# Causal attention on one core: a group's four score products in a row, the next job's maxima products in one lump behind them

## The chip, the cores and the metric

The kernel runs on one core of a Trainium2 chip. The metric is the device time of one execution in microseconds (us), as the median of several. TensorE (PE in the rows) has two columns of work in the trace, the matmuls (PE) and the weight loads (PEld); VectorE is DVE, ScalarE is ACT, GpSimd is POOL, and SyncE (SP) issues most transfers.

## What is computed

The reference is a small transformer: differential causal attention over x of 2 x 1024 x 128 (16 heads, each with two score maps), a routed feed-forward block, a second attention inside each token, and the feed-forward block again. The change is in the first attention only:

```
att = jnp.einsum('bhtd,bhsd->bhts', q, k) * (1.0 / math.sqrt(hd))
causal = jnp.tril(jnp.ones((T, T), dtype=bool))
att = jnp.where(causal, att, -jnp.inf)
att = jax.nn.softmax(att, axis=-1)
...
att = att[:, :, 0] - lambda_full * att[:, :, 1]
out = jnp.einsum('bhts,bhsd->bhtd', att, v)
```

## The kernel before

The program is a row of phases: `phase_a1` (projections), `phase_a2` (the first attention), `phase_a3`, `phase_f`, `phase_b` (the second attention) and `phase_f` again. Each phase begins when the one ahead of it is done. Within a phase every engine has its own list of instructions, written out by hand and run in that order; engines meet only at semaphores.

`phase_a2` does 16 **jobs**, one for each set of four score maps (index hh, 0 to 3) and batch element. A job needs the maximum of each score row before it can take exponentials, so the scores are computed twice. One pass, with queries on the partitions, gives the maxima (function `maximum_scores`, L449, with a product that adds the causal mask, L453); VectorE reduces it (L564). The negated maxima are split in three bf16 parts by GpSimd (`split`) and turned on TensorE (`maximum_rows`, L462), and VectorE adds them to the queries' tile as extra rows (L580). The other pass, with keys on the partitions, gives scores that have the maximum taken off already (`scores`, L492). ScalarE takes their exponential (L547), GpSimd clears the upper triangle of diagonal blocks (L384), and `values` (L505) multiplies them with v, four maps side by side in four column strips of the array. ScalarE copies the sums (L537), TensorE turns them (`turn`, L471), VectorE divides (L592, L594), and GpSimd combines.

A job has G = 12 **groups**, called at 0 to 11 here: four blocks of 128 keys for the first 512 queries, then eight for the second 512. A group is four score products, one for each hh, and one call of `values`, for the group before it. The score products have 512, 384, 256, 128 columns in groups 0 to 3, 512 in groups 4 to 8, then 384, 256 and 128. `scores` uses three PSUM banks in turn (ST_SLOTS = 3), so a product waits until the exponential three products back is done:

```
if s >= ST_SLOTS:
    pe.wait_ge(exp_done.sem, s - ST_SLOTS + 1)
```

The passes for later jobs are cut in **items**: 24 units of maxima for a job, u0 to u23 (u0 to u7 cover two maps each, with 128 to 512 columns for each; u8 to u23 cover one map with 640, 768, 896 or 1024 columns), one item of rows, and one turn. A job's list (`items`) has 26: u7 to u12 of the next job, the turn of the job before, u13 to u23, then u0 to u4 of the job after next, the rows, u5 and u6. Items use two pairs of PSUM banks in turn, so an item waits until VectorE is done with the item two back:

```
if i >= 2:
    pe.wait_ge(item_taken.sem, i - 1)
```

The loop of the tensor block that the diff touches deals the items out among the score products. VectorE takes the items in the same order, and makes the next keys' tiles (`pad`, L573) between them.

Of the kernel before, what the change touches and what calls it, by code (L numbers as in the profile page):

```python
# [301 lines left out]
def phase_a2(nc, rows_q, rows_k, rq, rk_of_group, rk, v1, att, k, queries_spread, keys_spread):  # L302
# [5 lines left out]
    with ExitStack() as ctx:  # L308
# [12 lines left out]
        U, G = len(units), len(groups)  # L321
        STEPS = 4 * G
# [21 lines left out]
        def items(n):  # L344

            later = [("max", n + 1, u) for u in range(0 if n < 0 else EARLY, U) if n + 1 < JOBS]
            if n >= 1:
                later.insert(min(TURN_ITEM, len(later)), ("turn", n - 1, 0))
            early = [("max", n + 2, u) for u in range(EARLY) if n + 2 < JOBS]
            if n + 1 < JOBS:  # L350
                early.insert(min(EARLY_ROWS, len(early)), ("rows", n + 1, 0))
            return later + early
# [80 lines left out]
        def _(pe):  # L433
# [40 lines left out]
            def item(kind, n, u):  # L474
                if kind == "max":
                    maximum_scores(n, u)
                elif kind == "rows":
                    maximum_rows(n)
                else:
                    turn(n)  # L480

            def scores(n, at, hh):
                g, b = n // BATCH, n % BATCH
                half, sbk = groups[at]
                s = STEPS * n + 4 * at + hh
                if at == 0 and hh == 0:
                    pe.wait_ge(rows_added.sem, n + 1)
                if s >= ST_SLOTS:
                    pe.wait_ge(exp_done.sem, s - ST_SLOTS + 1)
                lo, hi = queries_of(half, sbk)  # L490
                dst = ps[:, ST_BANK + s % ST_SLOTS]
                nc.tensor.matmul(dst[:, 0:hi - lo], rk[:, n % 3, hh, sbk * P:(sbk + 1) * P], rq[:, g, b, lo:hi],  # L492
                                 start=True, stop=True).then_inc(st_psum.sem, 1)

            def values(n, at):
                g, b = n // BATCH, n % BATCH
                half, sbk = groups[at]
                pe.wait_ge(exp_done.sem, exp_done.at(n, 4 * at + 4))
                if at in DIAGONAL:
                    pe.wait_ge(masked.sem, masked.at(n, DIAGONAL.index(at) + 1))  # L500
                if sbk == 0 and (n >= 1 or half == 1):
                    pe.wait_ge(o_copied.sem, 2 * n + half)
                lo, hi = queries_of(half, sbk)
                for hh in range(4):
                    last = nc.tensor.matmul(ps[32 * hh:32 * hh + 32, O_BANK, lo - 512 * half:512],  # L505
                                            v1[:, b * NT + sbk, 2 * g + hh // 2, :], ex[:, (G * n + at) % 3, hh, 0:hi - lo],
                                            start=sbk == 0, stop=sbk == (3 if half == 0 else NT - 1))
                last.then_inc(values_done.sem, 1)
# [4 lines left out]
            for n in range(JOBS):  # L513
                todo = items(n)
                given = 0
                for at in range(G):
                    for hh in range(4):
                        scores(n, at, hh)
                        while given < len(todo) and given * STEPS < (4 * at + hh + 1) * len(todo):
                            if todo[given][0] == "turn" and at < 2:  # L520
                                break
                            item(*todo[given])
                            given += 1
                    if at >= 1:
                        values(n, at - 1)
                    elif n >= 1:
                        values(n - 1, G - 1)
# [797 lines left out]
```

## Time and profile before

| what | value |
|---|---|
| median of 3 runs | 2138.11 us (2136.7 to 2138.21) |
| the profiled execution | 2138.5 us, its span 2136.7 us |
| busy over the span: PE, DVE, POOL, ACT | 86%, 88%, 66%, 52% |
| `phase_a2`'s jobs 0 to 14 | about 87 to 556 us of the span |
| job 15 of `phase_a2` | about 556 to 585 us |
| `phase_b` | about 700 to 2090 us |

The page's shares are means over stages with different limits. In `phase_b` VectorE is busy 99% of the time; it is not touched. A matmul's record lasts longer than the array is taken by it, because its end is modelled with the time in which results drain; the distance from one start to the next shows how long it occupies the array.

### The profile page before, as it was taken

To read this page: it belongs to the slowest core of one execution; us is meant where nothing else is said; L and a number is where in the kernel's file an instruction comes from. 1 tells how busy PE (TensorE), PEld (TensorE's weight loads), DVE (VectorE), ACT (ScalarE), POOL (GpSimd) and SP (SyncE) were. 2 spreads that over 40 slices of the span, in tenths; PEclk is the share of its full clock that TensorE was granted. 3 is DMA by queue.
4 is the path that set the end of the run, shared out by engine and by line. 5 is a ranking of instruction groups with operands and counts; after the bars stand their busy time and mean duration, and the time that the engine had idled before them with its cause. 6 is when DMAs were issued, how large, how long until landed. Compare 5 with 4: busy or idle time off the path is not lost. (4 is left out here: it accounts for less than half of the span.)

```text
span 2136.7 us, 35583 instructions
## 1 busy us (share of the span) xinstructions
PE 1847.3 (86%) x14162; PEld 1368.3 (64%) x14226; DVE 1884.3 (88%) x1607; ACT 1108.5 (52%) x1448; POOL 1414.5 (66%) x661
## 2 busy tenths in 40 slices
PE   2799999999756699898998998988989989889877
PEld 1344444444244578777787787777877877778776
DVE  6978887887254899999999999999999999999973
ACT  2267776776611355554545555545455555454540
POOL 5122222222201789889899898898998988989961
PEclk9899999999965899999999999999999999999996
DMA  3300000000000000000000000000000000000000
GB/s 100 64 5 8 8 6 8 9 5 2 1 0 0 1 1 1 2 1 2 1 1 2 1 1 2 1 1 2 1 1 2 1 1 1 2 1 1 1 1 20
DMA packets 10981, 14.46 MB, mean 7 GB/s; under 512 B 4656, under 2 KB 7632, under 8 KB 10672
## 3 DMA queue, kind: packets, MB, share of 16 engines
q1 hardware_dynamic: 9264, 11.31, 2.2%
q8 instruction: 126, 2.06, 0.4%
q10 hardware_dynamic: 1536, 0.63, 0.1%
q14 instruction: 55, 0.45, 0.1%
HBM read 4.57 MB, written 1.05 MB: 3 GB/s over the span
## 5 line engine op out<-in xcount | busy, mean ns | idle before, releaser
L1057 POOL TENSOR_TENSOR b_p_ring<-b_p_ring,b_m 128x2048 f32<-128x2048 f32 (+7 forms) x384 | 1250.9, 3299 | 139.9 <-DVE b_p_ring L969 137.9
L1095 ACT ACTIVATE b_p_ring<-b_p_ring 128x2048 f32<-128x2048 f32 (+7 forms) x384 | 532.7, 1412 | 640.8 <-POOL b_p_ring L1057 640.8
L1158 PE MATMUL b_ps<-k_ident,b_ev_ring 128*128 128x128 f32 (+6 forms) x4608 | 579.7, 276 | 121.7 <-DVE b_ev_ring L1015 121.5
L1015 DVE TENSOR_TENSOR b_ev_ring<-b_p_ring,b_ps 128x2048 f32<-128x2048 f32 (+7 forms) x384 | 634.1, 1655 | 1.7 <-ACT b_p_ring L1095 1.7
L969 DVE TENSOR_TENSOR b_p_ring<-b_ps,b_key 128x2048 f32<-128x2048 f32 (+7 forms) x384 | 634.4, 1660 | 0.0
L1158 PEld LDWEIGHTS b_ps<-k_ident,b_ev_ring 128*128 128x128 f32 (+6 forms) x4608 | 491.3, 135 | 183.3 <-DVE b_ev_ring L1015 159.1
L1158 PE MATMUL b_ps<-k_ident,b_p_ring 128*128 128x128 f32 (+6 forms) x4608 | 567.9, 273 | 19.5 <-ACT b_p_ring L1095 12.5
L1158 PEld LDWEIGHTS b_ps<-k_ident,b_p_ring 128*128 128x128 f32 (+6 forms) x4608 | 504.7, 135 | 26.1 <-ACT b_p_ring L1095 12.8
L564 DVE TENSOR_REDUCE a_negm<-a_ps 128x1 f32<-128x768 f32 (+7 forms) x384 | 354.5, 954 | 89.4 <-PE a_ps L453 88.1
L547 ACT ACTIVATE a_ex<-a_ps 128x512 f32<-128x512 f32 (+3 forms) x768 | 334.3, 497 | 189.3 <-PE a_ps L492 174.9
L384 POOL TENSOR_SCALAR_AFFINE_SELECT a_ex<-a_ex 128x512 f32<-128x512 f32 x128 | 81.6, 638 | 364.4 <-ACT a_ex L547 363.9
L449 PE MATMUL a_ps<-rk,rq 128*128 128x512 bf16 (+3 forms) x738 | 186.5, 332 | 37.2 <-DVE rk L573 16.7
L492 PE MATMUL a_ps<-rq,rk 128*128 128x512 bf16 (+3 forms) x734 | 204.5, 327 | 10.2 <-ACT a_ex L547 6.6
L505 PE MATMUL a_ps<-a_ex,v 128*32 128x512 f32 (+3 forms) x1536 | 164.6, 500 | 5.5 <-POOL a_ex L384 5.4
L492 PEld LDWEIGHTS a_ps<-rq,rk 128*128 128x128 bf16 x768 | 64.0, 97 | 154.2 <-ACT a_ex L547 124.8
L1123 PE MATMUL b_ps<-k_wqkv,b_xt 128*128 128x512 f32 x256 | 141.2, 635 | 5.5 <-DVE b_kmin L978 2.4
L449 PEld LDWEIGHTS a_ps<-rk,rq 128*128 128x128 bf16 x768 | 64.6, 98 | 94.1 <-DVE a_negm L564 48.3
L453 PE MATMUL a_ps<-k_mask,k_ident_b 128*128 128x128 bf16 x512 | 92.9, 223 | 0.0
L453 PEld LDWEIGHTS a_ps<-k_mask,k_ident_b 128*128 128x128 bf16 x512 | 49.9, 100 | 44.7 <-issue 3.2
L1124 PEld LDWEIGHTS b_ps<-bias,ones 3*128 3x128 bf16 x128 | 11.7, 91 | 102.0 <-issue 102.0
L505 PEld LDWEIGHTS a_ps<-a_ex,v 128*32 128x32 f32 x1536 | 30.4, 108 | 40.2 <-ACT a_ex L547 19.6
L976 DVE TENSOR_TENSOR_SCAN b_kmax<-k_reset_max,b_ps 128x512 f32<-128x512 bf16 x32 | 38.9, 1215 | 15.2 <-PE b_ps L1124 15.2
(163 smaller groups left out, 1065.6 us busy)
## 6 DMA issues: line engine op xcount, KB each, us to landing
rk_of_group<-rows_k SPq DMA_DIRECT2D x96, 32.0 KB, 2.0
rq<-rows_q SPq DMA_DIRECT2D x42, 64.0 KB, 2.3
k_wqkv<-in_wqkv SPq DMA_DIRECT2D x1, 2048.0 KB, 8.4
out<-x_all SPq DMA_DIRECT2D x4, 256.0 KB, 2.4
k_wo<-in_wo SPq DMA_DIRECT2D x1, 512.0 KB, 9.2
rq<-rows_q SPq DMA_DIRECT2D x12, 32.0 KB, 1.9
k_w_attn<-in_w_attn ACTq DMA_DIRECT2D x1, 192.0 KB, 2.8
k_reset_max<-in_reset_max ACTq DMA_DIRECT2D x1, 128.0 KB, 4.9
```

Source lines behind the costliest of these rows:

```text
L449: nc.tensor.matmul(dst[:, 512 * at + c:512 * at + c + w], rq[:, g, b, t * P:(t + 1) * P], rk[:, n % 3, hh, c:c + w], start=True, stop=c + ...
L453: last = nc.tensor.matmul(dst[:, c:c + P], k["ident_b"][:], k["mask"][:], start=False, stop=True)
L492: nc.tensor.matmul(dst[:, 0:hi - lo], rk[:, n % 3, hh, sbk * P:(sbk + 1) * P], rq[:, g, b, lo:hi], start=True, stop=True).then_inc(st_psum ...
L505: last = nc.tensor.matmul(ps[32 * hh:32 * hh + 32, O_BANK, lo - 512 * half:512], v1[:, b * NT + sbk, 2 * g + hh // 2, :], ex[:, (G * n + a ...
L547: nc.scalar.activation(ex[:, (G * n + at) % 3, hh, 0:hi - lo], ps[:, ST_BANK + s % ST_SLOTS, 0:hi - lo], ACT.Exp).then_inc(exp_done.sem, 1)
L564: nc.vector.tensor_reduce(negm[:, n % 2, t, heads[0]:heads[-1] + 1], src, X, ALU.max, negate=True).then_inc(item_taken.sem, 1)
L969: nc.vector.tensor_tensor(chunk(p_ring, c), over_rows(ps[:, Q_BANK], c), over_queries(key[:, buf, j0:j0 + ROWS, :], c), ALU.mult).then_inc ...
L1015: nc.vector.tensor_tensor(chunk(ev_ring, c), chunk(p_ring, c), over_queries(values(c), c), ALU.mult).then_inc(ev_done.sem, 1)
L1057: nc.gpsimd.tensor_tensor(pc, pc, over_rows(m[:, half].rearrange("p i h -> p (i h)"), c), ALU.subtract).then_inc(shifted.sem, 1)
L1095: nc.scalar.activation(pc, pc, ACT.Exp).then_inc(exp_done.sem, 1)
L1123: nc.tensor.matmul(ps[:, bank], xt[:, buf], k["wqkv"][:, i, cols], start=True, stop=False)
L1158: last = nc.tensor.matmul(ps[0:width, bank, b // IB * P:(b // IB + 1) * P], rows[:, r, b:hi].rearrange("p i h -> p (i h)"), k["ident"][:], ...
```

## The change

The items are no longer dealt out after each score product. They are dealt out only behind the fourth of a group, as many as keep pace with the groups.

```diff
@@ -516,7 +516,7 @@
                 for at in range(G):
                     for hh in range(4):
                         scores(n, at, hh)
-                        while given < len(todo) and given * STEPS < (4 * at + hh + 1) * len(todo):
+                        while hh == 3 and given < len(todo) and given * G < (at + 1) * len(todo):
                             if todo[given][0] == "turn" and at < 2:
                                 break
                             item(*todo[given])
```

With 26 items in a job (jobs 1 to 13), groups 0 and 6 have three items and the others two, before and after the change; job 0 has no turn, and its one group of three is group 0. Job 14 has 19 items, at most two in a group, and job 15 only a turn. The lists of the other engines, and the order of the items, are the same in both kernels. Nothing is added or removed.

First place, on TensorE, group 0 of a job (here job 1). L492 is a score product, L449 with L453 behind it are the products of one item, and L505 is `values`. Before:

```order
L492 MATMUL a_ps<-rq,rk 128x512
L449 MATMUL a_ps<-rk,rq 128x512 x2
L453 MATMUL a_ps<-k_mask,k_ident_b 128x128 x2
L492 MATMUL a_ps<-rq,rk 128x512
L449 MATMUL a_ps<-rk,rq 128x512
L449 MATMUL a_ps<-rk,rq 128x128
L453 MATMUL a_ps<-k_mask,k_ident_b 128x128
L492 MATMUL a_ps<-rq,rk 128x512 x2
L449 MATMUL a_ps<-rk,rq 128x512
L449 MATMUL a_ps<-rk,rq 128x128
L453 MATMUL a_ps<-k_mask,k_ident_b 128x128
L505 MATMUL a_ps<-a_ex,v 32x128 x4
```

And after:

```order
L492 MATMUL a_ps<-rq,rk 128x512 x4
L449 MATMUL a_ps<-rk,rq 128x512 x2
L453 MATMUL a_ps<-k_mask,k_ident_b 128x128 x2
L449 MATMUL a_ps<-rk,rq 128x512
L449 MATMUL a_ps<-rk,rq 128x128
L453 MATMUL a_ps<-k_mask,k_ident_b 128x128
L449 MATMUL a_ps<-rk,rq 128x512
L449 MATMUL a_ps<-rk,rq 128x128
L453 MATMUL a_ps<-k_mask,k_ident_b 128x128
L505 MATMUL a_ps<-a_ex,v 32x128 x4
```

Between the first and the third item there were three score products; now there is only the second item.

Second place, on TensorE, group 6 of the same job, the other one with three items. Before:

```order
L492 MATMUL a_ps<-rq,rk 128x512
L449 MATMUL a_ps<-rk,rq 128x512
L449 MATMUL a_ps<-rk,rq 128x384
L453 MATMUL a_ps<-k_mask,k_ident_b 128x128
L492 MATMUL a_ps<-rq,rk 128x512
L449 MATMUL a_ps<-rk,rq 128x512 x2
L453 MATMUL a_ps<-k_mask,k_ident_b 128x128
L492 MATMUL a_ps<-rq,rk 128x512 x2
L449 MATMUL a_ps<-rk,rq 128x512 x2
L453 MATMUL a_ps<-k_mask,k_ident_b 128x128
L505 MATMUL a_ps<-a_ex,v 32x512 x4
```

And after:

```order
L492 MATMUL a_ps<-rq,rk 128x512 x4
L449 MATMUL a_ps<-rk,rq 128x512
L449 MATMUL a_ps<-rk,rq 128x384
L453 MATMUL a_ps<-k_mask,k_ident_b 128x128
L449 MATMUL a_ps<-rk,rq 128x512 x2
L453 MATMUL a_ps<-k_mask,k_ident_b 128x128
L449 MATMUL a_ps<-rk,rq 128x512 x2
L453 MATMUL a_ps<-k_mask,k_ident_b 128x128
L505 MATMUL a_ps<-a_ex,v 32x512 x4
```

The fourth score product stood behind two items; now it stands right behind the three whose banks it shares.

## Rows read from the trace of the kernel before

**Rows 1.** Busy time and granted clock by window, jobs 0 to 14:

```profile
core 0: us, PE busy (x) PEld busy (x) DVE busy (x) ACT busy (x) POOL busy (x), PEclk, DMA share, GB/s
87.00:556.00 469.00, 446.65 (x3501) 193.19 (x3558) 374.31 (x454) 326.05 (x749) 107.31 (x223) 1.00 0.04 8
```

**Rows 2.** Timeline of PE: first score product of two jobs, one after another:

```profile
start us, us, engine line op out<-in xcount [idle before <-releaser]
303.86 0.39 PE L492 MATMUL a_ps<-rq,rk 128*128 128x512 bf16 x1
...
335.00 0.39 PE L492 MATMUL a_ps<-rq,rk 128*128 128x512 bf16 x1
```

**Rows 3.** Timeline of PE, same job, group 9 and the start of 10:

```profile
328.41 0.34 PE L492 MATMUL a_ps<-rq,rk 128*128 128x384 bf16 x1
...
329.83 1.06 PE L505 MATMUL a_ps<-a_ex,v 128*32 128x512 f32 x8
330.82 0.28 PE L492 MATMUL a_ps<-rq,rk 128*128 128x256 bf16 x1
```

**Rows 4.** Waits in jobs 0 to 15 (90 to 582 us), engine and what released it:

```profile
PEld a_ps L492 <- ACT a_ex L547: 124.8, 205, 0.9
...
PEld a_ps L449 <- DVE a_negm L564: 33.5, 80, 0.8
```

**Rows 5.** Timeline of job 15, a group of 512 columns:

```profile
569.68 0.82 PE L492 MATMUL a_ps<-rq,rk 128*128 128x512 bf16 x3
570.11 2.06 ACT L547 ACTIVATE a_ex<-a_ps 128x512 f32<-128x512 f32 x4 [0.33 <-PE a_ps L492]
...
570.76 0.39 PE L492 MATMUL a_ps<-rq,rk 128*128 128x512 bf16 x1 [0.26 <-ACT a_ex L547]
...
571.08 1.07 PE L505 MATMUL a_ps<-a_ex,v 128*32 128x512 f32 x8
572.08 0.33 PEld L492 LDWEIGHTS a_ps<-rq,rk 128*128 128x128 bf16 x3 [0.84 <-ACT a_ex L547]
```

**Rows 6.** Timeline of PE in job 15, groups of 384 and 256 columns:

```profile
576.87 0.66 PE L492 MATMUL a_ps<-rq,rk 128*128 128x384 bf16 x3
577.79 0.34 PE L492 MATMUL a_ps<-rq,rk 128*128 128x384 bf16 x1 [0.26 <-ACT a_ex L547]
...
579.06 0.50 PE L492 MATMUL a_ps<-rq,rk 128*128 128x256 bf16 x3
579.82 0.28 PE L492 MATMUL a_ps<-rq,rk 128*128 128x256 bf16 x1 [0.26 <-ACT a_ex L547]
```

**Rows 7.** Timeline of PE, group 0 and the first score product of 1:

```profile
306.11 0.45 PE L449 MATMUL a_ps<-rk,rq 128*128 128x512 bf16 x2 [0.34 <-DVE a_negm L564]
...
306.90 0.50 PE L492 MATMUL a_ps<-rq,rk 128*128 128x384 bf16 x2
```

**Rows 8.** Timeline of ACT at the same place: the copy and the exponentials behind it:

```profile
307.03 0.59 ACT L537 COPY a_o_sb<-a_ps 128x512 f32<-128x512 f32 x1 [0.36 <-PE a_ps L505]
307.51 1.65 ACT L547 ACTIVATE a_ex<-a_ps 128x384 f32<-128x384 f32 x4
```

**Rows 9.** Groups by form, 90 to 582 us: exponentials and two sizes of reduction:

```profile
line engine op names shapes xcount | busy us, mean ns | idle before us <-releasers
L547 ACT ACTIVATE a_ex<-a_ps 128x512 f32<-128x512 f32 x382 | 204.7, 607 | 65.7 <-PE a_ps L492 52.1 <-remote 12.6
...
L564 DVE TENSOR_REDUCE a_negm<-a_ps 128x1 f32<-128x1024 f32 x60 | 70.6, 1218 | 8.7 <-PE a_ps L453 8.7
L564 DVE TENSOR_REDUCE a_negm<-a_ps 128x1 f32<-128x896 f32 x60 | 63.9, 1084 | 3.0 <-PE a_ps L453 3.0
```

**Rows 10.** Timeline: an item's last product, and its reduction:

```profile
307.51 0.22 PE L453 MATMUL a_ps<-k_mask,k_ident_b 128*128 128x128 bf16 x1
...
307.76 0.83 DVE L564 TENSOR_REDUCE a_negm<-a_ps 128x1 f32<-128x640 f32 x1 [0.25 <-PE a_ps L453]
```

**Rows 11.** Timeline of PE, same job, first products of groups 6 and 7, and a turn:

```profile
310.54 1.04 PE L471 MATMUL a_ps<-k_ident,a_o_sb 128*128 128x128 f32 x8
...
319.23 0.39 PE L492 MATMUL a_ps<-rq,rk 128*128 128x512 bf16 x1
...
322.85 0.60 PE L492 MATMUL a_ps<-rq,rk 128*128 128x512 bf16 x2
```

**Rows 12.** Granted clock in job 15 and around the end of job 14:

```profile
565.00:580.00 15.00, 12.48 (x74) 3.05 (x74) 0.00 (x0) 12.97 (x28) 2.11 (x4) 1.00 0.00 1
550.00:555.00 5.00, 2.54 (x19) 1.34 (x20) 0.10 (x1) 0.45 (x2) 2.37 (x7) 0.75 0.00 0
```

**Rows 13.** Timeline of PE there, `values` behind a wait:

```profile
552.46 1.48 PE L505 MATMUL a_ps<-a_ex,v 128*32 128x384 f32 x8 [3.94 <-POOL a_ex L384]
```

## The prediction

> **What bounds the kernel now.** I read the windows first. The change touches only the tensor block of the first attention, so what matters is the stretch of its jobs 0 to 14, 469 us long [rows 1]. There PE's records cover 446.65 us, 95%, DVE's 374.31 (80%), ACT's 326.05 (70%), and the granted clock is 1.00, the 2.4 GHz level. The other phases wait for this one and then do what they did, so a microsecond more here is a microsecond more in the end.
>
> The 95% overstates how full the array is, since records include draining. So I read the PE timeline by starts. One job takes 335.00 - 303.86 = 31.14 us [rows 2]. What the array must stream in it, from the program's sizes at 2.4 GHz (512 columns take 0.213 us): scores 18,432 columns, 7.68 us; values 4,608 columns with four f32 passes and the four maps side by side, 7.68; maxima and masks 22,528 columns, 9.39; rows 0.43; the turn about 0.87 (its record of 1.04 [rows 11] less 0.17 of draining, by which the 0.39 of a 512-column record exceeds 0.213 too). Sum 26.05. Each group also loses about 0.25 around `values`: in job 15 the fourth score starts at 570.76 and `values` at 571.08, 0.107 more than one stream, and `values` takes 1.00 to the next score, 0.147 more than 0.853 [rows 5]. Group 9 confirms it: 2.41 from 328.41 to 330.82, where streams make 2.13 [rows 3]. So 26.05 + 12 x 0.25 = 29.05 is a job without a stall, and 31.14 - 29.05 = **2.1 us a job** is what PE stalls today. The waits name the causes: score products on exponentials, items on reductions [rows 4]. These figures are those of the weight-load column, whose waits start ahead of the array's own, so they give the kind and not the size.
>
> **The change, part by part.** Nothing is added or removed and no other engine's list moves. Only the distance changes between a PE instruction and what it waits for.
>
> *The fourth score in a row.* There are three score banks, so the fourth waits for the first one's exponential. Job 15 has hardly any items and so runs this very order already. There the first three scores start from 569.68, the exponentials at 570.11, and the fourth score at 570.76, which is 1.08 after the first, where three streams would be 0.64: a wait of 0.44 [rows 5]. The parts agree: 0.43 until the exponential starts, 0.607 for it [rows 9], 0.05 to the release. For 384 columns it is 577.79 - 576.87 = 0.92 against 0.48, again 0.44; for 256 columns 0.76 against 0.32, 0.44 [rows 6]. A narrower product streams sooner but its exponential is shorter too, so I take 0.44 for all 12 groups: 12 x 0.44 = 5.3 us a job. Items cannot fill it, because all of them stand behind the fourth score. In groups 1 and 5 the copy of the sums runs first on ACT: the exponential starts 307.51 - 306.90 = 0.61 after the first score instead of some 0.4 [rows 7, 8], 0.2 more each, 0.4 a job.
>
> *The third item of a lump.* There are two pairs of item banks, so the third item waits for the reduction of the first. In group 0 the lump starts 1.08 + 0.21 = 1.3 after the group's start. u7 streams 0.53 (1,280 columns), to 1.83. Its reduction starts about 0.2 later, since the mask's record starts 0.05 before the stream's end and the reduction 0.25 after that record's start [rows 10], and takes 1.22 [rows 9]: to 3.26, and 0.05 for the release, 3.3. u8 streams 0.32, so PE is ready at 2.15 and waits 1.17. In group 6, u19 (896 and 128 for the mask, 0.43) is streamed at 1.73 and reduced in 1.08 [rows 9], to 3.0; u20 streams 0.48 to 2.21; u21 waits for 0.87. Together 2.05 us a job.
>
> *The second item of a lump* waits for the second item of the last lump. In between PE has `values` (1.1 with its losses), four scores with their stall (1.3) and a first item (0.48), 2.9 us in a group of 512 columns. Both reductions of the last lump are done 0.2 + 2 x 1.22 - 0.48 = 2.2 us after its stream's end: it fits, with room for one `pad` or two. Behind the rows item, where the addition takes 1.2 and the group is short, I get 0.05 of wait at most. No cost. `values` and the mask of GpSimd come late enough as now.
>
> *What is given back.* The 2.1 us a job of today's stalls: both kinds exist only because of the present spacing, and all of them are replaced by the ones just counted.
>
> Net for a job of 26 items: 5.3 + 0.4 + 2.05 - 2.1 = 5.65 us. Jobs 0 to 13: 14 x 5.65 = 79. (Job 0 lacks the lump of group 6; left in, 0.9 too much.) Job 14 has no lump of three but hardly any stall besides its wait of 3.94 for a mask [rows 13], which stays, since it hangs on the last reduction; the last two maxima items there are now back to back, which moves that reduction 0.2 or so back. 12 x 0.44 + 0.4 - 0.2 = 5.5. Job 15: the turn stands behind the fourth score instead of the first, so one group gets the stall: 0.4. Sum 85, less 0.9: **84 us**. The profiled execution took 2138.5 us, 1.8 beyond its span; 2138.5 + 84 = 2222.5. That execution is 0.4 above the median of the runs, so the forecast stands for the median too: **2223 us**, 3.9% slower.
>
> **Bounds of the unknown.** The fourth score's wait is shown on the chip by job 15, but only without items. Its lower end is what remains if a group's stall shrank to today's total, 2.1 / 12 = 0.18; nothing in the trace does that. The third item's wait has no row in this form. From below it is nothing, if the reduction somehow were early; the nearest row from above is the wait of today, 0.34 in group 0 with two scores more ahead of the third item [rows 7]. Those are two streams of 0.43 and some waiting of their own; taking them away lengthens the wait, so my 1.17 is nearer than nothing.
>
> **Rivals.**
> *Only the score wait shows.* The reductions hide. For it: DVE is idle 20% of the stretch. Against it: PE runs its list in order and u9 needs the pair of banks that u7 holds. Time: 3.6 x 14 = 50, with 5.5 and 0.4 for the last jobs 56: 2194 us.
>
> *The clock falls.* For it: around the end of job 14 the clock was 0.75, and behind the wait of 3.94 `values` took 1.48 for 384 columns [rows 12, 13], where 512 take 1.06 at full clock [rows 3]. Against it: in job 15, with four scores in a row, stalls of 0.4 in each group, and PE busy 12.48 of 15 us, it was 1.00 [rows 12]; the waits of 1.17 are far from 3.94. If the granted clock were 0.9 in the whole stretch, 26 us of streams become 28.9: 2.9 x 14 = 40 more, 2263 us.
> The Trainium skill, "TensorE: Matmul & The Clock Gate", section "A second HAM failure mode: psum-queue depth-cycling", says that short idle times of TensorE between groups of matmuls, in a kernel that cycles through PSUM banks each iteration, can make the clock swing between its two levels. This kernel does cycle through banks, so by that rule the time would come out near this rival's; job 15's 1.00 speaks against it.
>
> *Faster.* Four products in a row and all items in one dense stretch remove the 2.1 us a job of stalls and bring no others: 2138.5 - 15 x 2.1 = 2107 us. The place is the fourth score of each group, and the price that decides is 0.18 us a group: below it the change gains, above it the change loses, if lumps of three cost nothing. For it: today most waits of PE are of just these two kinds [rows 4], so another spacing might suit. Against it: 0.44 in every width [rows 5, 6].
> The Trainium skill, "Perfetto Trace Analysis", section "Matmul Optimizations", says that the matmul engine scales its power with use and that it is therefore important to execute matmuls back to back in batches. That speaks for the change. By this rule the lumps could only help, up to this rival's time; but the granted clock is 1.00 already [rows 1], so the trace leaves it nothing to win.
>
> *The change does nothing*, because each group has the same sum of work and the engines would even it out: 2138. Against it: the list's order decides when a wait is met, and it is met in order.
>
> **How the numbers follow.** Score wait and third-item wait both as worked out: 0.80, with a range of its own of 2207 to 2238, from 5.65 a job give or take 1 (0.1 us on the fourth score of each group is 1.2 a job). Only the score wait: 0.08. The clock: 0.06. Faster: 0.03. Nothing: 0.03. The time named is that of the first. The range that leaves out no more than 2 in 10 reaches down to the second case, 2190, and up to 2250, part of the way to the clock's. A measurement of this kernel can tell about 0.2%, 4 us, from no change. Faster by more than that 0.03, within it 0.03, slower 0.94.
>
> **What the profile of the changed kernel would show.** A job of 36.8 us between first score products, where it was 31.14. Group 9, free of stalls now, 2.85 instead of 2.41. Group 0 at 4.1 and group 6 at 4.7, where group 6 had 322.85 - 319.23 = 3.62 [rows 11]. In the waits, PE's score products behind exponentials with some 0.26 us and more before nearly every fourth, and in groups 0 and 6 an L449 behind a reduction with about 1 us. The clock at 1.00. Wrong would be: a fourth score that starts without a wait because its bank is free; a third item without one; a granted clock under 0.97 in this stretch; or a new wait of `values` on a mask in ordinary jobs, which would add to the sum.

## The result, and the profile after

The changed kernel takes 2217.93 us (median of 4 runs, 2217.17 to 2226.42) against 2137.4 us for the kernel before (median of 4); the ratio is 1.039, 95% interval 1.0361 to 1.042. The forecast was 2223, with a range from 2190 to 2250: inside, and 5 us off.

The profiled execution has a span of 2216.1 us, 79.4 more than before. Start with the windows, as before the change. This is the stretch of jobs 0 to 14, which now ends at about 642 us, and then the stretch from the start of `phase_a3` to VectorE's first multiplication in `phase_b` (L969), called **the light stretch** here, since no engine is busy for much more than half of it:

```profile
core 0: us, PE busy (x) PEld busy (x) DVE busy (x) ACT busy (x) POOL busy (x), PEclk, DMA share, GB/s
87.00:642.00 555.00, 474.48 (x3560) 187.69 (x3558) 373.61 (x454) 311.84 (x749) 106.57 (x223) 1.00 0.03 7
674.30:784.60 110.30, 60.55 (x285) 46.43 (x285) 59.37 (x71) 17.39 (x25) 8.74 (x3) 0.67 0.00 0
```

VectorE's busy time is that of [rows 1] to 0.7 us, spread over 86 us more. ScalarE has as many instructions as before, and its exponentials of 512 columns take 606 ns in the mean (607 before); its busy time is 14 us lower because records that overlap are counted once, and more do now. The granted clock is still 1.00. So nothing became slower by itself; engines wait more.

The PE timeline of a whole job, cut to the groups that the prediction spoke of (answers to [rows 2, 7] for the job and group 0):

```profile
start us, us, engine line op out<-in xcount [idle before <-releaser]
306.94 0.82 PE L492 MATMUL a_ps<-rq,rk 128*128 128x512 bf16 x3
308.01 0.39 PE L492 MATMUL a_ps<-rq,rk 128*128 128x512 bf16 x1 [0.26 <-ACT a_ex L547]
308.24 0.59 PE L449 MATMUL a_ps<-rk,rq 128*128 128x512 bf16 x2
308.67 0.28 PE L453 MATMUL a_ps<-k_mask,k_ident_b 128*128 128x128 bf16 x2
308.78 0.43 PE L449 MATMUL a_ps<-rk,rq 128*128 128x512 bf16 x2
309.05 0.22 PE L453 MATMUL a_ps<-k_mask,k_ident_b 128*128 128x128 bf16 x1
310.26 0.45 PE L449 MATMUL a_ps<-rk,rq 128*128 128x512 bf16 x2 [0.99 <-DVE a_negm L564]
310.55 0.22 PE L453 MATMUL a_ps<-k_mask,k_ident_b 128*128 128x128 bf16 x1
310.69 0.43 PE L505 MATMUL a_ps<-a_ex,v 128*32 128x128 f32 x8
311.05 0.66 PE L492 MATMUL a_ps<-rq,rk 128*128 128x384 bf16 x3
312.22 0.34 PE L492 MATMUL a_ps<-rq,rk 128*128 128x384 bf16 x1 [0.51 <-ACT a_ex L547]
...
325.28 0.82 PE L492 MATMUL a_ps<-rq,rk 128*128 128x512 bf16 x3
...
328.37 0.60 PE L449 MATMUL a_ps<-rk,rq 128*128 128x512 bf16 x2 [0.70 <-DVE a_negm L564]
...
329.96 0.82 PE L492 MATMUL a_ps<-rq,rk 128*128 128x512 bf16 x3
...
336.17 0.66 PE L492 MATMUL a_ps<-rq,rk 128*128 128x384 bf16 x3
337.09 0.34 PE L492 MATMUL a_ps<-rq,rk 128*128 128x384 bf16 x1 [0.26 <-ACT a_ex L547]
...
339.01 0.50 PE L492 MATMUL a_ps<-rq,rk 128*128 128x256 bf16 x3
...
343.96 0.82 PE L492 MATMUL a_ps<-rq,rk 128*128 128x512 bf16 x3
```

Read the starts. The fourth score of group 0 comes 308.01 - 306.94 = 1.07 us after the first, where three streams are 0.64. In group 1, behind the copy on ScalarE, it comes 1.17 after, where three streams are 0.48. The third item of group 0 starts 1.2 us after the mask of the second; a mask needs 0.05. Group 0 takes 4.11 us (to 311.05), where it was 3.04 [rows 2, 7]. Group 6 takes 4.68, where it was 3.62 [rows 11], and group 9 takes 2.84, where it was 2.41 [rows 3]. The job takes 37.02 us, from 306.94 to 343.96, where it was 31.14. The idle times in brackets are measured from the modelled end of the record before them, so they are shorter than what the array loses (0.26 for 0.43).

The waits over the stage, by engine and releaser (90 to 670 us; answers to [rows 4]):

```profile
PEld a_ps L492 <- ACT a_ex L547: 205.1, 299, 0.9
PE a_ps L492 <- ACT a_ex L547: 56.2, 192, 0.6
...
PEld a_ps L449 <- DVE a_negm L564: 29.7, 27, 1.2
PE a_ps L449 <- DVE a_negm L564: 23.0, 27, 1.0
```

Score products now wait 192 times on PE itself for an exponential. 16 jobs of 12 groups make 192 fourth products, and each of them waits (this window starts behind the first of them and has one wait of a third product, in job 15). Items wait 27 times for a maxima reduction: two for each of 13 jobs and one for job 0. These are the two waits of the prediction. The only other wait of PE that adds up to more than 1 us is that of `values` on a mask, three times as before: 0.5, 4.3 and 0.6 us now, 0.9, 3.9 and 0.6 before, all from job 14 on.

### The profile page after: what moved, and what is told of

Read it like the earlier page. It is cut to its first block and busy times, and to the rows that moved or that the text cites. A ratio compares the mean times of both kernels' runs of the same rounds, so it can differ in the third digit from the quotient of the medians.

```text
span 2216.1 us, 35647 instructions
## 1 busy us (share of the span) xinstructions
PE 1869.3 (84%) x14226; PEld 1362.9 (62%) x14226; DVE 1883.9 (85%) x1607; ACT 1094.0 (49%) x1448; POOL 1413.2 (64%) x661
## 5 line engine op out<-in xcount | busy, mean ns | idle before, releaser
L969 DVE TENSOR_TENSOR b_p_ring<-b_ps,b_key 128x2048 f32<-128x2048 f32 (+7 forms) x384 | 637.0, 1667 | 0.0
L547 ACT ACTIVATE a_ex<-a_ps 128x512 f32<-128x512 f32 (+3 forms) x768 | 317.8, 498 | 268.5 <-PE a_ps L492 268.4
L492 PE MATMUL a_ps<-rq,rk 128*128 128x512 bf16 (+3 forms) x768 | 192.3, 331 | 57.3 <-ACT a_ex L547 56.4
L492 PEld LDWEIGHTS a_ps<-rq,rk 128*128 128x128 bf16 x768 | 57.9, 97 | 265.6 <-ACT a_ex L547 205.9
L449 PE MATMUL a_ps<-rk,rq 128*128 128x512 bf16 (+3 forms) x768 | 180.1, 334 | 47.8 <-DVE a_negm L564 30.0
L505 PE MATMUL a_ps<-a_ex,v 128*32 128x512 f32 (+3 forms) x1536 | 164.3, 500 | 5.3 <-POOL a_ex L384 5.3
L1123 PE MATMUL b_ps<-k_wqkv,b_xt 128*128 128x512 f32 x256 | 136.3, 614 | 5.5 <-DVE b_kmin L978 2.4
L449 PEld LDWEIGHTS a_ps<-rk,rq 128*128 128x128 bf16 x768 | 63.7, 99 | 78.3 <-DVE a_negm L564 43.3
L453 PE MATMUL a_ps<-k_mask,k_ident_b 128*128 128x128 bf16 x512 | 92.1, 223 | 0.0
L453 PEld LDWEIGHTS a_ps<-k_mask,k_ident_b 128*128 128x128 bf16 x512 | 49.9, 100 | 44.8 <-issue 3.4
L1124 PEld LDWEIGHTS b_ps<-bias,ones 3*128 3x128 bf16 x128 | 11.6, 91 | 98.2 <-issue 98.2
L505 PEld LDWEIGHTS a_ps<-a_ex,v 128*32 128x32 f32 x1536 | 30.3, 108 | 36.6 <-issue 18.8
L1124 PE MATMUL b_ps<-bias,ones 3*128 3x512 bf16 x128 | 49.5, 386 | 0.0
```

The lines of the kernel that those rows point to most:

```text
L449: nc.tensor.matmul(dst[:, 512 * at + c:512 * at + c + w], rq[:, g, b, t * P:(t + 1) * P], rk[:, n % 3, hh, c:c + w], start=True, stop=c + ...
L453: last = nc.tensor.matmul(dst[:, c:c + P], k["ident_b"][:], k["mask"][:], start=False, stop=True)
L547: nc.scalar.activation(ex[:, (G * n + at) % 3, hh, 0:hi - lo], ps[:, ST_BANK + s % ST_SLOTS, 0:hi - lo], ACT.Exp).then_inc(exp_done.sem, 1)
L969: nc.vector.tensor_tensor(chunk(p_ring, c), over_rows(ps[:, Q_BANK], c), over_queries(key[:, buf, j0:j0 + ROWS, :], c), ALU.mult).then_inc ...
L1123: nc.tensor.matmul(ps[:, bank], xt[:, buf], k["wqkv"][:, i, cols], start=True, stop=False)
```

## The experiments

Each ratio is against the kernel before, run beside it on the same chip. The changed kernel's 2217.93 comes from another session, in which the kernel before took 1.3 us more than beside the first four experiments. The phases behind the attention also shift a total by a few us (last section). So the start of `phase_a3` in the traces (674.3 us in the changed kernel) is given too: what a change in the attention stage is worth is read there. Line numbers move by a few where an experiment adds lines.

**The lump one score earlier.** All items of a group stand behind the third score, so that they cover the first exponential.

```diff
-                        while hh == 3 and given < len(todo) and given * G < (at + 1) * len(todo):
+                        while hh == 2 and given < len(todo) and given * G < (at + 1) * len(todo):
```

> All items of a group behind its third score product instead of its fourth; everything else as in the changed kernel. The fourth product then has the whole lump between it and the first one's exponential. Theory (fourth score waits 0.44 in each group, third item of a lump waits for a reduction): the 5.7 us a job of the fourth score go, the third item's wait of about 2 stays, and with shorter groups VectorE with its pads gets tight: a job of 31 to 32.5 us, 2135 to 2160 us in all, within 1% of the kernel before. Rival (the lump itself costs, since items come too fast for the reductions, and the four products in a row cost little): the time stays above 2180.

Measured: 2148.93 us (2148.08 to 2149.9), against 2136.06 before, ratio 1.0059 (1.0042 to 1.0076). One move by one score product, with the items still in a lump, takes back 68 of the 80 us; `phase_a3` starts at 602.3, 72 us sooner. Its timeline shows what is left: the waits of the third item of group 0, of the second item of group 5 and of the third item of group 6:

```profile
311.03 0.82 PE L492 MATMUL a_ps<-rq,rk 128*128 128x512 bf16 x3
311.68 0.59 PE L449 MATMUL a_ps<-rk,rq 128*128 128x512 bf16 x2
...
313.71 0.45 PE L449 MATMUL a_ps<-rk,rq 128*128 128x512 bf16 x2 [0.99 <-DVE a_negm L564]
313.99 0.22 PE L453 MATMUL a_ps<-k_mask,k_ident_b 128*128 128x128 bf16 x1
314.05 0.38 PE L492 MATMUL a_ps<-rq,rk 128*128 128x512 bf16 x1
...
325.15 0.55 PE L449 MATMUL a_ps<-rk,rq 128*128 128x512 bf16 x2 [0.25 <-DVE a_negm L564]
...
329.34 0.60 PE L449 MATMUL a_ps<-rk,rq 128*128 128x512 bf16 x2 [0.70 <-DVE a_negm L564]
...
343.31 0.82 PE L492 MATMUL a_ps<-rq,rk 128*128 128x512 bf16 x3
```

The fourth score (314.05) starts right behind the item ahead of it. The third items wait as in the changed kernel, 0.99 and 0.70. A second item (325.15, group 5) waits 0.25 too: once the scores' stall is gone, groups are short enough for the reductions and pads to show there. A job takes 343.31 - 311.03 = 32.28 us. So without the fourth score's wait a job is 4.7 us shorter and not 5.7. Against the bare work that the prediction's figures give for each group, 0.45 us are lost in group 5 and 0.33 in group 11, where the second item waits for the addition of the rows (L580); 0.16 are lost in group 1. That is the difference. That the lump itself is the main cost is refuted; its third items still cost 2 us a job.

**The third item behind `values`.** Four scores in a row stay, but no lump has three.

```diff
+                    first = given
...
-                        while hh == 3 and given < len(todo) and given * G < (at + 1) * len(todo):
+                        while hh == 3 and given < len(todo) and given * G < (at + 1) * len(todo) and given < first + 2:
...
                         values(n - 1, G - 1)
+                    while given < len(todo) and given * G < (at + 1) * len(todo):
+                        item(*todo[given])
+                        given += 1
```

> As the changed kernel, but lumps of at most two items: the third item of groups 0 and 6 stands behind the values products. Theory: values (1.1 us in group 6, 0.46 in group 0) covers 0.7 of the 0.7 to 0.9 wait in group 6 and 0.46 of the 1.0 to 1.2 in group 0, so 1.2 to 1.3 us a job, about 2200 us, 17 us below the changed kernel. Rival (the third item's wait is hidden or costs nothing): no difference, 2218.

Measured: 2201.46 us (2199.9 to 2202.87), ratio 1.0304 (1.0287 to 1.0322), 16.5 below the changed kernel; `phase_a3` starts at 656.2, 18.1 sooner. The wait of group 6 is covered and that of group 0 is down to this:

```profile
338.28 0.45 PE L449 MATMUL a_ps<-rk,rq 128*128 128x512 bf16 x2 [0.64 <-DVE a_negm L568]
```

That the total met the expected 2200 is in part luck. A job is 1.57 us shorter (35.46), not 1.2 to 1.3: group 0 loses 0.45, as expected, group 6 0.86, where 0.7 was, and group 1 loses 0.26, which the expectation had left out. With an item between `values` and group 1, its fourth score comes 0.91 after its first, as in groups without a copy. Against that, job 15 and the end of the stage take 33.7 us, where they took 31.8. The edit also moves job 15's only item, the turn, from group 2 to behind `values` of group 0, where it waits 1.29 us for a copy of ScalarE. The granted clock from 622 to 632 us was 0.81, where it was 1.00 in the changed kernel at the same place (642 to 652):

```profile
625.65 1.89 PE L471 MATMUL a_ps<-k_ident,a_o_sb 128*128 128x128 f32 x8 [1.29 <-ACT a_o_sb L541]
```

**Two short reductions.** The maxima of u7 and u19 are taken over 128 columns of each map only, so part of the maxima is left out.

```diff
-                src = item_banks(i).rearrange("p (h c) -> p h c", h=len(heads))[:, :, 0:(t + 1) * P]
+                width = P if u in (7, 19) else (t + 1) * P
+                src = item_banks(i).rearrange("p (h c) -> p h c", h=len(heads))[:, :, 0:width]
```

> As the changed kernel, but the reductions of u7 and u19, for which the third items wait, read only the first 128 columns of each map: a part of the maxima is left out, so the time tells only of the wait. Theory: both waits of the third item vanish (1.17 and 0.87 as worked out, 2.0 a job over 14 jobs): about 2190 us. Rival (the third item's wait is not what the reductions set, or the score products would take it up again): less than 8 us gained.

Measured: 2199.58 us (2197.92 to 2202.28), ratio 1.0297 (1.028 to 1.0315), 18.4 below the changed kernel; `phase_a3` starts at 652.8, 21.5 sooner. That is a gain of the right kind that falls short of the expected 28. The timeline of PE in group 0 shows why:

```profile
333.33 0.82 PE L492 MATMUL a_ps<-rq,rk 128*128 128x512 bf16 x3
...
335.86 0.45 PE L449 MATMUL a_ps<-rk,rq 128*128 128x512 bf16 x2 [0.19 <-DVE a_negm L565]
336.14 0.22 PE L453 MATMUL a_ps<-k_mask,k_ident_b 128*128 128x128 bf16 x1
...
336.65 0.66 PE L492 MATMUL a_ps<-rq,rk 128*128 128x384 bf16 x3
```

Group 0 takes 3.32 instead of 4.11. Some wait is left, since even the short reduction (two maps of 128) takes time: the expectation had left it out. 0.79 less in group 0 is 1.22 less the 0.42 of a reduction of 256 elements. Group 6 lost 0.80, from 4.68 to 3.88.

**The first exponential shortened.** ScalarE takes the first exponential of each group over 128 columns only, in jobs 1 to 15; the rest of those exponentials is left out.

```diff
                         lo, hi = queries_of(half, sbk)
+                        if n >= 1 and hh == 0:
+                            hi = lo + P
                         nc.scalar.activation(ex[:, (G * n + at) % 3, hh, 0:hi - lo], ps[:, ST_BANK + s % ST_SLOTS, 0:hi - lo],
```

> As the changed kernel, but in jobs 1 to 15 the first exponential of each group covers only 128 columns, the rest of that map's exponentials is left out. A 512-column exponential took 607 ns, a 128-column one 276, so by the theory the fourth score's wait shrinks from 0.44 to 0.11 in six groups, by 0.22 in two and by 0.11 in two more: 2.6 us a job over 14 jobs, and in job 15: about 2178 us. Rival (the fourth score waits for something else, such as the array's draining or the weight loads): no difference, 2218.

Measured: 2185.37 us (2182.76 to 2188.61), ratio 1.023 (1.0213 to 1.0247), 32.6 below the changed kernel, where about 40 were expected. In the traces the stage up to the start of `phase_a3` is 35 us shorter (639.3 against 674.3). The PE timeline of a group of 512 columns (group 4) now has all four scores in one piece, and ScalarE beside it:

```profile
307.08 1.15 PE L492 MATMUL a_ps<-rq,rk 128*128 128x512 bf16 x4
307.51 1.79 ACT L549 ACTIVATE a_ex<-a_ps 128x128 f32<-128x128 f32 x4 [1.38 <-PE a_ps L492]
```

Four scores in 1.15 us, where the record from the first start to the fourth end was 308.01 + 0.39 - 306.94 = 1.46: the 0.31 is near the 0.33 by which the exponential is shorter (607 and 276 ns). So the fourth score waits for the first exponential, and that wait shrinks with it. A job is 2.43 us shorter (34.60) and not the expected 2.6; most of the difference is in group 5, where the fourth score comes 0.32 sooner but the group is only 0.20 shorter. The rest of the shortfall lies outside jobs 1 to 13.

**Other ways to deal the items.** Both experiments start from the kernel before. The first item of a group stands behind the third score (in the other kernel behind the second), the second behind the fourth, and a third one behind `values`; groups with three items are 8 and 9. (Only in group 9 are all items small; group 8 gets u22 and u23, the widest, and u0.)

```diff
+                share = [2] * 8 + [3, 3, 2, 2] if len(todo) > 24 else [2, 2, 1, 2, 1, 2, 2, 1, 2, 1, 2, 1] if len(todo) > 1 else [0, 0, 1]
+                places = [(at, i) for at in range(len(share)) for i in range(share[at])]
...
-                        while given < len(todo) and given * STEPS < (4 * at + hh + 1) * len(todo):
-                            if todo[given][0] == "turn" and at < 2:
-                                break
+                        if given < len(todo) and places[given] == (at, hh - 2):
                             item(*todo[given])
                             given += 1
...
+                    while given < len(todo) and places[given] == (at, 2):
+                        item(*todo[given])
+                        given += 1
```

The other kernel has `(hh - 1) / 2` for `hh - 2`.

> Another dealing of the same items: the first item of a group behind its third score product, the second behind its fourth, a third one behind values, and the groups with three are 8 and 9, where items are small, instead of 0 and 6. Theory (PE stalls are only the fourth score's and the near items' waits): both are gone but for some 0.3 of the copies in groups 1 and 5, so a job comes near the 29.05 us of work: 29.3 to 30.3 us, 13 to 25 us below the kernel before, 2111 to 2124 us. Rival (VectorE's own list, 25.4 us a job, binds in some groups whatever the spacing, as in the run with the lump behind the third product, where a job took 32.3): no faster than the kernel before, 2136 or above.

> As the run before in this list, but the first item stands behind the second score product. Between the first and the fourth score then lie two streams and an item, 0.64 + 0.32 to 0.53, against the 1.08 that the first exponential takes: a fourth score's wait of 0 to 0.1 in groups with small items. Theory: 0 to 1 us a job behind the run above, 2113 to 2135 us. Rival: VectorE binds, 2136 or above.

Measured: 2130.04 us (2127.82 to 2133.8), ratio 0.9967 (0.9954 to 0.9979), and 2129.78 us (2125.17 to 2131.16), ratio 0.9955 (0.9941 to 0.9968). Both beat the kernel before by 8 us, or 0.4%; the intervals leave out no difference. The first misses the 13 to 25 us that were expected of it, and its rival (no gain) is out too; the second is within its expectation. The two can't be told apart. VectorE does not bind to the point of undoing the gain. `phase_a3` starts at 581.2 and 580.8, where it was 588.0: 7 of the 8 us are in this stage. In the first, a job takes 330.43 - 299.72 = 30.71 us, 1.7 above the 29.05 of work:

```profile
299.72 0.82 PE L492 MATMUL a_ps<-rq,rk 128*128 128x512 bf16 x3
...
301.92 0.69 PE L492 MATMUL a_ps<-rq,rk 128*128 128x384 bf16 x3
302.44 0.43 PE L449 MATMUL a_ps<-rk,rq 128*128 128x512 bf16 x2
302.71 0.22 PE L453 MATMUL a_ps<-k_mask,k_ident_b 128*128 128x128 bf16 x1
303.14 0.34 PE L492 MATMUL a_ps<-rq,rk 128*128 128x384 bf16 x1 [0.21 <-ACT a_ex L550]
...
304.74 0.50 PE L492 MATMUL a_ps<-rq,rk 128*128 128x256 bf16 x3
...
330.43 0.82 PE L492 MATMUL a_ps<-rq,rk 128*128 128x512 bf16 x3
```

Group 0 takes 2.20, 0.03 more than the bare work by the prediction's figures (2.17). Group 1 takes 2.82 against 2.38 of work. There the exponentials are late behind the copy, and the fourth score waits although an item stands ahead of it. The rest is spread over other groups in pieces of up to 0.24; their causes were not taken apart.

**The changed kernel once more.**

> The changed kernel once more, beside the kernel before on one chip, to see how much of its 80 us is the attention stage (86 us there in the two traces) and how much the granted clock in the phases behind it gives back or takes: 2215 to 2228 us, the attention stage within 0.5 us of the first trace, the rest differing with the granted clock at the opening of the second attention. Rival (the later phases are shorter for a reason that the change brings with it): the opening of the second attention always runs at full clock in this kernel.

Measured: 2220.93 us (2219.06 to 2221.4), ratio 1.0386 (1.037 to 1.0402), beside 2138.24. `phase_a3` starts at 674.7 (674.3 in the first trace). The light stretch took 115.2 us, where the same kernel took 110.3 in the first trace:

```profile
674.70:789.90 115.20, 66.17 (x285) 47.52 (x285) 59.39 (x71) 17.49 (x25) 8.74 (x3) 0.62 0.00 0
```

VectorE's and ScalarE's busy times are the same to 0.1; PE's is 5.6 longer, at a granted clock of 0.62 instead of 0.67. The rival, that the opening of `phase_b` always runs at full clock in this kernel, is refuted.

## Why the prediction was right

**What bounds the kernel.** The split of a job's 31.14 us into bare work and stalls held in kind: group 9 went to 2.84 (forecast 2.85), and with the items dealt differently group 0 ran within 0.03 of its bare work. In size the work was put a little low. The prediction took 0.25 us a group beside the streams, from job 15, although its own check, group 9, showed 2.41 - 2.13 = 0.28. Groups without a wait, as 0, 3, 6 and 7 of the first other dealing, take 0.02 to 0.03 more than by its figures. So a job without a stall is nearer 29.3 than 29.05, and the kernel before stalled nearer 1.85 us a job than 2.1 (estimates, from these lengths).

**The fourth score.** Forecast 0.44 in each group, 0.2 more in groups 1 and 5. Measured 1.07 - 0.64 = 0.43 in group 0, 1.17 - 0.48 = 0.69 in group 1 and 1.27 - 0.64 = 0.63 in group 5, and one wait in each of 192 groups. Shown by taking the cause away in two ways: by place (the lump one score earlier) and by size (the short exponential).

**The third item.** Forecast 1.17 and 0.87 us. Measured by the groups' lengths, group 0 is at 4.11 (forecast 4.1) and group 6 at 4.68 (4.7), with 27 waits. Shown by the place of the third item and by the length of the reduction it waits for.

**The second item at no cost.** Right for the changed kernel. It holds only because the scores' stall stretches the groups; without that stall second items do wait, and most of the 1 us of the 5.7 a job that did not come back was lost there.

**The sum.** Jobs 1 to 13 took 31.14 us each before and 37.03 after, 5.89 more, where the forecast was 5.65. The step that was a little off is the 2.1 us of stalls given back, which were nearer 1.85 (above). Job 0, without the turn and the lump of group 6, took 29.75 and 34.55, 4.8 more (forecast 5.65 less 0.87). In all, jobs 0 to 13 grew by 81.3 us, the forecast was 78. Job 14 grew from 34.6 to 39.4 (its first score stands at 521.86 and 603.17, the next job's at about 556.5 and 642.56), 4.8, forecast 5.5. The prediction took it as free of stalls but for the mask's, but groups 1 and 4 are as long after as before (3.09 and 2.69): they had the stall already. Job 15 and the end of the stage took 0.2 more, forecast 0.4. In all the stage is 86.3 us longer; the forecast was 84.

**What was off** is the step "a microsecond more here is a microsecond more in the end". The stage gave 86.3, the span 79.4. Of the missing 6.9, 5.4 lie in the light stretch (115.7 before, 110.3 after) and 1.5 behind it: the last stretch of the program took 10.0 us, where it had taken 11.6. That the total came within 5 us of the forecast is in part luck: the stage was 2.3 above its forecast and the rest gave 6.9 back.

The repeated run has 86.7 in the stage, 115.2 us in the light stretch and a span of 2219.6, 82.9 more than before. So the 5 us of the first trace there are not a gain of the change, for the same kernel did not have them again. It has 3.8 us missing too: 0.6 in the light stretch and 3.2 in the last 80 us. Here are the end of `phase_b` (from VectorE's last multiplication on) and the end of the program, before and then in the repeated run (columns as in the first table):

```profile
2058.70:2079.50 20.80, 15.66 (x125) 14.74 (x123) 8.53 (x11) 10.41 (x11) 5.45 (x3) 0.92 0.00 1
2125.10:2136.70 11.60, 7.43 (x48) 5.89 (x48) 3.46 (x5) 2.30 (x4) 0.00 (x0) 0.69 0.32 90
...
2144.90:2164.10 19.20, 14.12 (x125) 13.20 (x123) 8.50 (x10) 10.35 (x11) 5.39 (x3) 1.00 0.00 1
2209.60:2219.60 10.00, 5.68 (x48) 5.11 (x48) 3.46 (x6) 2.01 (x4) 0.00 (x0) 0.92 0.37 105
```

The same products take less at a higher granted clock: 1.00 for 0.92, and 0.92 for 0.69. A kernel whose items are dealt differently (first item behind the second score) took 20.8 and 11.6 us there, like the kernel before, so a new order does not by itself bring the higher clock. The kernel before has one trace only; whether it too has executions with the shorter end is not known.

**The rivals.** That only the score wait shows is out, by the 27 waits of items and the two experiments on the third item. That the clock falls in the stage is out: it stayed 1.00, although about 29 of a job's 37 us are work and PE idles for the rest, in pieces of 0.4 to 1.2 us. The rule on short idle times between groups of matmuls, in the Trainium skill, "TensorE: Matmul & The Clock Gate", section "A second HAM failure mode: psum-queue depth-cycling", was not borne out at this idling. That the change makes the kernel faster, or does nothing, is out by the 80 us.

## What to carry to other kernels

A ring of three buffers lets three producers run ahead, and the fourth in a row then waits for a whole round trip, here 1.08 us from the first product's start to the fourth's. Put independent work between the last product that the ring takes and the first that must wait, as much as the round trip less what streams anyway; behind it the same work hides nothing. When several items use a ring of two, count them in a lump: the third waits for the full service of the first, whatever the mean load of that engine is (VectorE was idle a third of this stage). To price such a reordering, look for a place in the trace where the new order already runs; here the last job, which has only a turn beside its scores, gave the fourth score's wait to 0.01 us.

## What was not expected of the hardware

The same kernel, in two executions with stages of equal length up to there (674.3 and 674.7 us), took 110.3 and 115.2 us for the light stretch. Most of the difference is to be seen in TensorE's opening products of `phase_b`, f32 products of 512 columns with two records each. The first trace of the changed kernel:

```profile
764.53 1.12 PE L1123 MATMUL b_ps<-k_wqkv,b_xt 128*128 128x512 f32 x2 [1.00 <-ACT b_xt L1084]
765.90 1.13 PE L1123 MATMUL b_ps<-k_wqkv,b_xt 128*128 128x512 f32 x2
```

And its repeated run:

```profile
766.41 2.08 PE L1123 MATMUL b_ps<-k_wqkv,b_xt 128*128 128x512 f32 x2 [1.00 <-ACT b_xt L1084]
768.95 1.97 PE L1123 MATMUL b_ps<-k_wqkv,b_xt 128*128 128x512 f32 x2
```

1.12 and 2.08 us are the two levels of the clock, 2.4 and 1.2 GHz, for the same instruction behind the same wait: the granted clock is 1.00 from 764.5 to 767 us in the first trace, and 0.53 from 766.4 to 771 in the second. Of nine traces of this study, the stretch took 110.3 us in two (the first of the changed kernel and that with the short exponential) and 115.1 to 115.8 in seven. What decides between them was not settled; the program of these phases is the same in all. The last 80 us of the program varied by up to 3.3 us between the traces as well. The first four runs of the changed kernel went from 2217.17 to 2226.42 us, at mean granted clocks of 0.963 and 0.956; where the slowest lost its time is not known, since it has no trace. For differences of some us between kernels that means: compare the touched stage in the traces, not only the totals.
